# A twelve-unit attention and expert kernel: the first unit's rows in pieces of four neighbouring heads, maxima of units 5 to 8 in quarters

## What is computed

```
# ffn layer (head size 8, rotary positions)
attn = softmax(rope(src@Wq) . rope(src@Wk_c@Wk) / sqrt(8)); sa = (attn @ (src@Wv_c@Wv)) @ Wo
x = rmsnorm(src + sa, norm1_w)
shared = swiglu(x @ W_shared_in) @ W_shared_out
routed = sum over the top 2 of 4 experts of the best of 2 groups: w_e * (swiglu(x @ W1_shared) @ W2_experts[e])
out = rmsnorm(x + shared + routed, norm2_w)
# attention layer (64 channels, head size 4)
out = softmax(q . k / sqrt(8)) @ v @ Wo.T + bo
```

## Time and profile before

| | |
|---|---|
| median of 3 runs | 874.33 us (873.68 to 875.46) |
| the profiled execution: whole time / span of the trace | 874.73 / 872.9 us |
| PE busy | 811.1 us, 93% |
| DVE busy | 673.0 us, 77% |
| ACT busy | 497.3 us, 57% |
| POOL busy | 332.5 us, 38% |
| PE's granted clock, mean | 0.972 |

### The profile page before, as it was taken

How to read it: one execution, slowest core, us unless ns; L and a number is a source line. 1 busy time by engine, 2 the same in 40 slices (tenths; PEclk the granted TensorE clock), 3 DMA queues, 4 the chain that set the end, 5 groups by cost and what they waited for, 6 DMA issues and landing times.

```text
span 872.9 us, 12671 instructions
## 1 busy us (share of the span) xinstructions
PE 811.1 (93%) x4144; PEld 294.9 (34%) x4144; DVE 673.0 (77%) x1296; ACT 497.3 (57%) x1042; POOL 332.5 (38%) x685
## 2 busy tenths in 40 slices
PE   3589999999999999999889999999999999999967
PEld 2133234433433332332313223233344343333333
DVE  5687998778759767876989998898987787682247
ACT  1045776356537645754777777767764575477320
POOL 2054325362543444345231613325153621522342
PEclk9578999999999999999999999999999999999989
DMA  3536232130120101010130331403311300000000
GB/s 103 154 85 148 73 63 54 27 72 3 46 32 1 39 11 32 6 43 12 21 76 6 76 77 39 101 16 92 59 39 36 83 10 1 4 13 3 1 12 13
DMA packets 27258, 38.92 MB, mean 45 GB/s; under 512 B 6949, under 2 KB 24965, under 8 KB 25573
## 3 DMA queue, kind: packets, MB, share of 16 engines
q1 hardware_dynamic: 25165, 36.39, 17.6%
q10 hardware_dynamic: 2028, 1.72, 0.8%
HBM read 28.01 MB, written 9.50 MB: 43 GB/s over the span
## 4 chain that ended last, share of the span: by engine, by line
PE 72%; DVE 18%; ACT 3%; issue 2%; DMA 2%; POOL 2%; ACTq 0%; POOLq 0%; SPq 0%; DVEq 0%
PE ps_out L682 17%; PE ps L668 14%; PE ps L649 13%; PE ps L744 11%; DVE maxes L820 11%; PE ps L729 6%; PE ps L631 2%; ACT probs L984 2%; PE ps L736 1%; PE ps L638 1%; DVE src L898 1%; PE ps L707 1%; DVE stats L779 1%; PE ps L720 1%; DVE src L791 1%
## 5 line engine op out<-in xcount | busy, mean ns | idle before, releaser
L984 ACT ACTIVATE probs<-ps 128x512 f32<-128x512 f32 x768 | 417.0, 597 | 249.3 <-PE ps L668 247.0
L820 DVE TENSOR_REDUCE maxes<-ps 128x1 f32<-128x512 f32 x768 | 482.9, 683 | 75.9 <-PE ps L649 74.2
L649 PE MATMUL ps<-k_aug,q_aug 72*128 72x512 bf16 (+1 forms) x768 | 259.6, 390 | 18.9 <-DMA k_aug<-ones_row 17.0
L668 PE MATMUL ps<-q_aug,k_aug 75*128 75x512 bf16 (+1 forms) x768 | 263.2, 383 | 5.3 <-DMA q_aug<-max_parts_rows 3.3
L682 PE MATMUL ps_out<-probs,v_aug 128*18 128x512 f32 x1536 | 203.1, 601 | 5.4 <-ACT probs L984 4.9
L649 PEld LDWEIGHTS ps<-k_aug,q_aug 72*128 72x128 bf16 (+1 forms) x768 | 66.0, 98 | 193.3 <-issue 123.3
L668 PEld LDWEIGHTS ps<-q_aug,k_aug 75*128 75x128 bf16 (+1 forms) x768 | 66.4, 97 | 149.9 <-issue 94.5
L744 PE MATMUL ps<-w,hidden 128*128 128x512 f32 x256 | 117.0, 596 | 0.0
L911 DVE TENSOR_TENSOR prod<-ps,gate 128x512 f32<-128x512 f32 x56 | 38.7, 692 | 58.3 <-PE ps L744 42.6
L1170 POOL TENSOR_TENSOR prod<-prod 128x512 f32<-128x512 f32 x28 | 35.5, 1268 | 97.0 <-DVE prod L911 93.8
L744 PEld LDWEIGHTS ps<-w,hidden 128*128 128x128 f32 x256 | 47.6, 190 | 51.3 <-issue 46.8
(11 more groups left out here) (121 smaller groups left out, 665.9 us busy)
## 6 DMA issues: line engine op xcount, KB each, us to landing
q_aug<-qk_parts SPq DMA_DIRECT2D x7, 1152.0 KB
k_aug<-qk_parts SPq DMA_DIRECT2D x21, 384.0 KB
qk_parts<-parts SPq DMA_DIRECT2D x45, 128.0 KB, 2.3
q_aug<-qk_parts SPq DMA_DIRECT2D x8, 288.0 KB
k_aug<-qk_parts SPq DMA_DIRECT2D x24, 96.0 KB
qk_parts<-parts SPq DMA_DIRECT2D x24, 64.0 KB, 2.0
...
```

Source lines behind the costliest of these rows:

```text
L649: pe.matmul(bank(use[0]), q_aug[p0:p1, r, at, qt * 128:(qt + 1) * 128], k_aug[p0:p1, r, at, :], start=True, stop=True).then_inc(bank_full[ ...
L668: pe.matmul(bank(use[0]), k_aug[p0:p1, r, at, kt * 128:(kt + 1) * 128], q_aug[p0:p1, r, at, :], start=True, stop=True).then_inc(bank_full[ ...
L820: dve.tensor_reduce(maxes[:, u % 2, qt, h:h + 1], full(use[0]), AX.X, ALU.max)\
L984: act.activation(probs[:, step % P_RING, c, :], full(use[0]), ACT.Exp, scale=scale)\
```

## The change

What it does:

- Unit 0: the columns of `wq` and `wk` are permuted, so that q and k come out with the four heads of a group next to each other (`position`; the same for all ffn units). q is loaded with one DMA a piece instead of three. The order is now: q of piece 0; k part by part, for piece 0 each part as soon as it is stored; q of pieces 1 to 3 once all k parts are stored. The rows of ones of unit 0 are set by one DMA at the start. The late loads begin when all rows of unit 0 have landed.
- All units: k's rows are loaded part by part, each part's rows written three times with a stride of three, instead of three copies of all parts. The rows of ones are loaded only where the buffer doesn't hold them yet (`new_ones`).
- Units 5 to 8 have their maxima in four pieces; `MAX_LATE`, the tables of `PREP` and `POST` and `HOLD` have new values. The tables of `POST` (not printed) move single steps by 0 to 12 places; ffn preparation is now split at places 35 and 48 instead of 31 and 45.
- `MAX_PAIRS` and `EXP_PAIRS` (two tiles of scores in one step) are empty sets: their code does nothing here, and its lines are left out.

```diff
-STACK_DMAS, FIRST_DMAS = 1 + PARTS + 1, 2 * PARTS + 1
-EARLY_UNITS = {0, 1}
+FIRST_DMAS = 1 + PARTS
+EARLY_UNITS = {0, 1, 5, 6, 7, 8}
...
-    return h if is_ffn(u) else HH * half_of(u, h) + h // 4 * 2 + h % 2
+    return 4 * (h // 8 * 2 + h % 2) + h % 8 // 2 if is_ffn(u) else HH * half_of(u, h) + h // 4 * 2 + h % 2
+
+
+def max_column(u, h):
+
+    return position(u, h) if is_ffn(u) else h
...
-    first, second = m // (2 * TT) // 2, m // (2 * TT) % 2
-    return 4 * first + second + 2 * (m % 2), m // 2 % TT
+    i = m // (2 * TT)
+    if max_pieces(u) == PIECES:
+        return 8 * (i // 4) + 4 * (i % 2) + i // 2 % 2 + 2 * (m % 2), m // 2 % TT
+    return 4 * (i // 2) + i % 2 + 2 * (m % 2), m // 2 % TT
 
 
 def stack_dmas(u):
-    return STACK_DMAS * row_halves(u) if u else FIRST_DMAS
+    return (1 + PARTS + new_ones(u)) * row_halves(u) if u else FIRST_DMAS
+
+
+def new_ones(u):
+
+    return u < AUG_RING or is_ffn(u) != is_ffn(u - AUG_RING)
...
-    return slice(8 * i, 8 * i + 8) if max_pieces(u) == 2 else slice(group_head(i, 0), 8 * (i // 2) + 8, 2)
+    n = H // max_pieces(u)
+    if is_ffn(u) or n == 8:
+        return slice(n * i, n * (i + 1))
+    return slice(group_head(i, 0), 8 * (i // 2) + 8, 2)
...
-PREP = {"norm_stats": [0], "norm_apply": [10], "x_transpose": [13], "qk_project": [19, 35], "qk_split": [31, 45],
-        "v_project": [27], "stack": [42, 56]}
-PREP_SECOND = {"norm_stats": [21], "norm_apply": [31], "x_transpose": [49], "qk_project": [53, 67],
-               "qk_split": [63, 77], "v_project": [66], "stack": [73, 88]}
-PREP_THIRD = {"norm_stats": [17], "norm_apply": [20], "x_transpose": [22], "qk_project": [24, 34],
-              "qk_split": [31, 52], "v_project": [25], "stack": [51, 52]}
+PREP_FIRST = {"norm_stats": [0], "norm_apply": [10], "x_transpose": [13], "qk_project": [19, 35], "qk_split": [35, 48],
+        "v_project": [31], "stack": [41, 48]}
+PREP = {"norm_stats": [0], "norm_apply": [10], "x_transpose": [13], "qk_project": [19, 35], "qk_split": [35, 48],
+        "v_project": [31], "stack": [41, 48]}
+PREP_SECOND = {"norm_stats": [25], "norm_apply": [34], "x_transpose": [48], "qk_project": [53, 63],
+               "qk_split": [62, 73], "v_project": [65], "stack": [77, 83]}
+PREP_THIRD = {"norm_stats": [16], "norm_apply": [18], "x_transpose": [22], "qk_project": [24, 33],
+              "qk_split": [30, 55], "v_project": [25], "stack": [43, 57]}
...
 PREP_ATTN = {"norm_stats": [7], "norm_apply": [11], "x_transpose": [15], "qk_project": [18, 35],
-             "qk_split": [31, 38], "v_project": [19], "stack": [34, 55]}
+             "qk_split": [25, 35], "v_project": [19], "stack": [38, 45]}
+PREP_THIRD_ATTN = {"norm_stats": [7], "norm_apply": [11], "x_transpose": [13], "qk_project": [18, 35],
+                   "qk_split": [31, 35], "v_project": [15], "stack": [36, 42]}
+PREP_LAST_ATTN = {"norm_stats": [7], "norm_apply": [12], "x_transpose": [15], "qk_project": [18, 36],
+                  "qk_split": [32, 43], "v_project": [19], "stack": [37, 52]}
...
-    at = PREP_SECOND if u == 1 else PREP_THIRD if u == 2 else PREP if is_ffn(u) else PREP_ATTN
+    at = {0: PREP_FIRST, 1: PREP_SECOND, 2: PREP_THIRD, 4: PREP_ATTN, 5: PREP_ATTN, 6: PREP_THIRD_ATTN, 7: PREP_LAST_ATTN}.get(u, PREP)
...
-MAX_LATE = [39, 36, 23, 12, 16, 18, 22, 19, 17, 15, 17, 20, 22]
+MAX_LATE = [39, 33, 23, 14, 16, 18, 22, 24, 25, 21, 18, 18, 22]
...
-HOLD = {"x_transpose": 29, "qk_project": 37, "v_project": 32, "heads_transpose": 26, "out_project": 23,
-        "x1_transpose": 29, "logits": 23, "shared_out": 35, "expert": 27, "max_rows": 26, "heads_out": 30,
+HOLD = {"x_transpose": 29, "qk_project": 37, "v_project": 32, "heads_transpose": 41, "out_project": 23,
+        "x1_transpose": 32, "logits": 32, "shared_out": 38, "expert": 33, "max_rows": 23, "heads_out": 27,
...
-            (wq[:, :], w["ffn_Wq"]),
+            (x1T[:, 0:C], w["ffn_Wq"]),
...
             for c in range(PARTS):
                 queue.wait_ge(part_done, PARTS * (2 * u + qk) + c + 1)
-                to = scratch_rows(u, qk)[:, c, :, :] if qk else scratch_rows(u, qk)[c, :, :, :]
-                queue.dma_start(to.rearrange("d h n -> h d n"), parts[0:H * head_dim(u), qk, c, :])\
-                    .then_inc(parts_stored[qk], 16)
+                landed = first_k_stored[c] if u == 0 and qk else parts_stored[qk]
+                queue.dma_start(scratch_rows(u, qk)[:, c, :, :].rearrange("d h n -> h d n"),
+                                parts[0:H * head_dim(u), qk, c, :]).then_inc(landed, 16)
+
+        def k_stored(engine):
+
+            for c in range(PARTS):
+                engine.wait_ge(first_k_stored[c], 16)
 
         def load_rows(queue, u, qk):
 
-            queue.wait_ge(parts_stored[qk], PARTS * 16 * (u + 1))
             d, r, halves, pieces = head_dim(u), u % AUG_RING, row_halves(u), stack_pieces(u)
+            n = H // halves // pieces
+            if u or qk == 0:
+                queue.wait_ge(parts_stored[qk], PARTS * 16 * (u + 1 - qk))
             for g, i in itertools.product(range(halves), range(pieces)):
-                landed = aug_loaded[r] if u else first_loaded[i]
-                r0, n = first_row(u, 2 * g), H // halves // pieces
-                at = slice(g * n, (g + 1) * n) if u else piece_heads(u, i)
+                r0, at = first_row(u, 2 * g), slice((g + i) * n, (g + i + 1) * n)
+                rows, landed = product_rows(u), aug_loaded[r] if u else first_loaded[i]
                 of = scratch_rows(u, qk)[:, :, at, :]
-                if qk == 0 and u:
-                    of = of.rearrange("c d h n -> (c d) h n").unsqueeze(1)
-                    queue.dma_start(q_aug[r0:r0 + product_rows(u), r, at, :], of.to_broadcast([PARTS * d, PARTS, n, S]))\
-                        .then_inc(landed, 16)
-                elif qk == 0:
-                    for s in range(PARTS):
-                        queue.dma_start(q_aug[s:product_rows(u):PARTS, r, at, :], of.rearrange("c d h n -> (c d) h n"))\
-                            .then_inc(landed, 16)
-                else:
-                    for s in range(PARTS):
-                        r1 = r0 + PARTS * d * s
-                        queue.dma_start(k_aug[r1:r1 + PARTS * d, r, at, :], of.rearrange("d c h n -> (d c) h n"))\
-                            .then_inc(landed, 16)
-                    r1 = r0 + product_rows(u)
-                    queue.dma_start(k_aug[r1:r1 + PARTS, r, at, :], ones_row[:, :, :].to_broadcast([PARTS, n, S]))\
-                        .then_inc(landed, 16)
+                if qk == 0:
+                    if u + i == 1 and i:
+                        k_stored(queue)
+                    of = of.rearrange("d c h n -> (d c) h n").unsqueeze(1)
+                    queue.dma_start(q_aug[r0:r0 + rows, r, at, :], of.to_broadcast([PARTS * d, PARTS, n, S])).then_inc(landed, 16)
+                    continue
+                for c in range(PARTS):
+                    if u + i == 0:
+                        queue.wait_ge(first_k_stored[c], 16)
+                    of_c = of[:, c, :, :].rearrange("d h n -> d (h n)").unsqueeze(1)
+                    queue.dma_start(k_aug[r0 + c:r0 + rows:PARTS, r, at, :], of_c.to_broadcast([d, PARTS, n * S])).then_inc(landed, 16)
+            if qk and u and new_ones(u):
+                for g in range(halves):
+                    n, r1 = H // halves, first_row(u, 2 * g) + product_rows(u)
+                    queue.dma_start(k_aug[r1:r1 + PARTS, r, g * n:(g + 1) * n, :], ones_row[:, :, :].to_broadcast([PARTS, n, S]))\
+                        .then_inc(aug_loaded[r], 16)
...
                     i, = args
+                    if i == 0:
+
+                        stacked(sp, 0)
                     sp.dma_start(*late[i]).then_inc(late_loaded, 16)
...
+                    elif n == 4:
+                        of = of.rearrange("c (j g) n -> c g j n", g=2)
+                        for g in range(2):
+                            p0, at = first_row(u, 2 * g) + product_rows(u), position(u, group_head(i, g))
+                            sp.dma_start(q_aug[p0:p0 + PARTS, r, at:at + 3:2, :], of[:, g, :, :]).then_inc(max_loaded[i], 16)
...
-                        seq(dve.tensor_copy(wk[:, :], ps_out[:, 0:C]))
+                        for a in range(2):
+                            c0 = a * C // 2
+                            seq(dve.tensor_copy(wk[:, c0:c0 + C // 2].rearrange("k (g c j) -> k g c j", g=2, c=4),
+                                                ps_out[:, c0:c0 + C // 2].rearrange("k (c g j) -> k g c j", g=2, c=4)))
...
+            for a in range(2):
+                c0 = a * C // 2
+                act.activation(wq[:, c0:c0 + C // 2].rearrange("k (g c j) -> k g c j", g=2, c=4),
+                               x1T[:, c0:c0 + C // 2].rearrange("k (c g j) -> k g c j", g=2, c=4), ACT.Copy).then_inc(wq_turned, 1)
             act.activation(identb[:, :], ident[:, :], ACT.Copy).then_inc(identb_set, 1)
```

(2 more changed lines are left out.)

182 lines of the change are left out of this document (119 added, 63 removed).

## The result

The changed kernel took 883.61 us as the median of four runs (879.73 to 885.50), beside 874.00 us (873.39 to 875.46) for the kernel before on the same chip: a ratio of 1.0104 with an interval of 1.0073 to 1.0136. It is slower, and outside the predicted range. The profiled execution took 885.50 us, its span is 883.7.

The account below looks back on a forecast made before the run. The prediction took PE as the main bound (72% of the chain, DVE 18%), with the start and some stages hanging on others. Terms -4.8, -2.0, -1.0 and -2.6 summed to -10.4 us, giving 863.9 us, range 858.0 to 871.5.

Parts of the forecast that it names:

- part D: Stages 5 to 10: maxima in quarters, moved out of stages that DVE bounds; -2.6 us, bounds -6 and +1.6.
- The other tables and HOLD: All stages: the remaining table and holding-time changes move steps by some places; counted as 0 us.
- the line on SP: SP's queue in four stages: 8 added groups hold it 3.5 us each, 28 of 202 us, where SP mostly waits.
- Start (A): Start up to PE's first maxima: store and loads freed of traffic; maxima at 27.5 instead of 32.31, gain 4.8 us.
- the bound of 1.4: Start: gain of 1.4 us with the old store and load durations (3.70 and 4.49 us); PE starts at 30.9.
- The cover of three us: Start: late loads end at 37 us, SP stores the first maxima at about 40; three us to spare.
- Stage 0 (B): Stage 0: norm applied two places earlier (20 to 18), less wait, clock kept; 2.0 us gained, bounds 0 and 4.7.
- Stages 1 and 2 (C): Stages 1 and 2: fewer maxima in stage 1 (78.4 to 75.0) relieve DVE; -1.0 us, bounds 0 and -3.
- The slower one: Stages 6 and 7: PE held for POOL's `max_parts` behind a split at four transpositions; 18 us, time 878, chance 0.05.
- The rival of slow first rows: Start: single-part reads written three times run at two thirds of the rate; gain only 2.5, 866.2 us, chance 0.10.
- the sum: Whole kernel: the parts' terms -4.8, -2.0, -1.0 and -2.6 add to -10.4 us.
- The best case of the start: Start: upper bound with a store of 2.0 and a load of 2.45 us; PE starts at 27.0, gain 5.3.

Follow-up runs that it names:

- the order put back: Changed kernel with FFN k loads at place 56 and `PREP_SECOND` and `MAX_LATE[1]` as before the change; 867.94 us, ratio 0.9898.
- the old tables: Changed kernel's code with PREP, POST, HOLD, `MAX_LATE` and `EARLY_UNITS` of the kernel before; 870.31 us, ratio 0.9908.
- the fastest kernel: The same kernel as the order put back: changed kernel with FFN k loads, `PREP_SECOND` and `MAX_LATE[1]` as before; 867.94 us, ratio 0.9898.
- more of the old balance: The fastest kernel with six `MAX_LATE` entries at or nearer old values and the old table for steps behind one unit's attention; 902.42 us, ratio 1.0298.
- the quarters alone: The old tables with only the maxima of units 5 to 8 in quarters and their new `MAX_LATE`; 872.26 us, ratio 0.9945.

## Why the prediction was wrong

**The step that failed** is the last of part D: "The other tables and HOLD move steps by some places; a step moved off a wait can land on another. At 0", together with the line on SP, which counted what each group holds the queue for (2.1 us of store, 1.5 of issue) and found 28 us in 202. Both look at the issuing queue. The k loads had moved from place 56 to 48 and the split with them; that they put 1.18 MB each in flight, and past which store they were moved, was not worked out, although the tables say it. Unit 9's maxima run over 61 places from place 21 of stage 8, its first half is due at place 51.5, and the k load now stands at 48; before, the half was due at 48 and the load stood at 56. Unit 10 in stage 9 is the same: due at 50 with the load at 48, before at 50.5 with the load at 56. Priced from rows 5 and rows 3, 1.18 MB at 173 GB/s last 6.8 us, and a store that has to wait for all of it takes up to 6.8 + 1.9 us instead of 1.9 (an estimate); measured 6.17 and 6.36. With the order put back, stages 8 and 9 gave back 8.4 us and stage 0 7.8 (115.7 to 107.9), together 16.2; the profiled spans differ by 17.8 (883.7 and 865.9), the rest of which lies mainly in the tail (47.2 and 45.0 us). In stage 0 the store is not all of it: with the store quick again, at 2.80 and 2.71 us, the stage still ended at 118.4 and 118.2 us, when PE waited 3.1 or 9.6 us for the rows of k instead, which were issued behind the store, and the clock fell.

**Start (A): right direction, too large.** PE's first maxima stood at 30.40 instead of the predicted 27.5 (before 32.31): a gain of 1.9 where 4.8 were forecast, near the bound of 1.4 that the old durations gave.

```profile
20.33 2.94 DMA qk_parts<-parts
...
23.30 0.73 ACTq L612
...
24.82 5.45 DMA k_aug<-qk_parts
...
30.40 0.60 PE ps L735
```

Two terms were mis-sized. Of the three k loads not one but all are behind the store on the chain (three issues of 0.7 us, from 23.30 on), for ACT issues its three stores first, in 2.44 us. And the load takes 5.45 us, not 2.45: pieces 1 to 3 are issued right behind and share the engines. Alone it took 3.22, which shows the cause, and with it that 2.45 was too little even so. The store took 2.94 (predicted 2.3). One gain was not foreseen: with neighbouring heads the row load of the maxima takes 1.69 to 1.73 us instead of 2.45 and is issued in 0.28 us instead of 0.77; so a group of unit 0 or 1 is 0.7 us shorter. The first exp scores came at 47.7 (with the old tables at 47.3) instead of 49.3; predicted was 44.5. The cover of three us for the first store was there: SP's fourth late load ended at 39.4, the store was issued at 43.10.

**Stage 0 (B): the effect came, not by the cause named.** In the fastest kernel the clock is 1.00 throughout from 60 to 100 us, as it was not in the earlier trace rows. But it is so with the old tables too, where the norm stands at its old place 20. The two places earlier were not what did it; stage 0 ends at 107.9 and 108.1. Start and clock together gave 4.4 us (predicted 6.8).

**Stages 1 and 2 (C): two thirds of the size.** -0.5 and -0.2 us, predicted -1.0 together with bounds 0 and -3. In the fastest kernel, which has `MAX_LATE[1]` of before, stage 1 took 80.0 us again, and nothing of C is left but 0.2 us in stage 2.

**Stages 5 to 10 (D): right where nothing collides.** In the fastest kernel stages 5 to 10 changed by -2.8, -0.9, -0.3, +1.9, +0.2 and +0.2, sum -1.7, predicted -2.6. The waits for rows in stage 5 went as forecast (none left in its waits view, before 1.9 us in the earlier trace rows), and stages 7 to 9 took 1.8 more where 2.0 was said. The 36 transpositions wait 13.5 us for POOL in all, where 28 waited 7.3. Not foreseen were stages 3 and 11, +0.4 and +1.4; together they take back all of D (+1.8). Stage 11 points at the table of the steps behind unit 10's attention: it took 59.1 us again with that table as before (in the kernel with more of the old balance), and 58.9 with the new `MAX_LATE` and all other tables old (in the profile of the quarters alone). The term that was put at 0 holds this loss too. Why stage 3 got longer is not known.

**The rivals.** The slower one named POOL as the place; the chip showed another, the DMA engines. The rival of slow first rows hung a loss of rate on the rule on the number of engines; the share fell by a third, the rate did not fall.

**How near the sum came.** The time of the fastest kernel, 867.94 us against 877.07 for before on its chip, is 9.1 us less; the sum had said 10.4. This is another kernel than the one forecast, and the nearness is in part luck: the profiled spans differ by 7.0 us (872.9 and 865.9), of which 4.4 lie in stage 0 and 2.3 in the tail, for which nothing was forecast. Nor is the tail steady: the kernel with only `MAX_LATE[1]` put back has the same code there and a tail of 48.1 us. In the 5 us that start 30 us before the end its clock was 0.53, that of the fastest kernel 0.77.

**Three slips of the working.** The best case of the start adds up to 22.53 + 2.0 + 0.2 + 2.45 = 27.2, not 27.0. The slower rival's 18 us on top of the forecast give 881.9 us, not 878. And beside the DMA share of 0.63 that was held against 12 of 16 engines, rows 5 have one of 0.78, which is over it. None of them moves the forecast.

**Left open:** why a store on a queue of its own starts to move only 4 us or more behind its issue when a large load is under way; why stage 3 is longer; whether `MAX_LATE[1]` matters.
